# Experts: inner rows weighed and their peaks taken tile by tile without the root, next rows rounded ahead of the results

## The reference, cut to what matters

```python
def rmsnorm(x, w, eps):
    return x * jax.lax.rsqrt(jnp.mean(jnp.square(x), axis=-1, keepdims=True) + eps) * w

def act_quant(x):
    scale = 127.0 / jnp.maximum(jnp.max(jnp.abs(x), axis=-1, keepdims=True), 1e-05)
    return jnp.clip(jnp.round(x * scale), -128, 127) / scale

def bitlinear(x, norm_w, w):
    xn = rmsnorm(x, norm_w, BIT_EPS)          # BIT_EPS = 1e-08
    xq = xn + jax.lax.stop_gradient(act_quant(xn) - xn)
    wq = w + jax.lax.stop_gradient(weight_quant(w) - w)
    return xq @ wq.T

def one_expert(w_col, gpn, gpw, dpn, dpw):
    ...
    h = bitlinear(xin, gpn, gpw)              # 512 rows x 256 -> 512 rows x 1024
    g, y = jnp.split(h, 2, axis=-1)
    out = bitlinear(jax.nn.silu(g) * y, dpn, dpw)   # 512 rows x 512 -> 512 rows x 256
    ...
```

## Time and profile before

| | us |
|---|---|
| median of 3 runs | 2300.96 (2299.19 to 2306.49) |
| the profiled execution | 2308.77 |
| its span | 2307.0 |
| the experts' second block in it, from the first DVE instruction on rows to the next stage | 1573.8 to 1780.2 |
| one expert in its loop, from DVE's L2449 to the next L2449 | 22.55 to 23.04 |
| VectorE busy over the span | 1558.2 (68%) |
| TensorE busy over the span | 1705.8 (74%) |

### The profile page before, as it was taken

One profiled execution on the slowest core, in us unless ns is written; L12 is line 12 of the kernel. 1 busy time (PEld: TensorE's weight loads), 2 busy tenths in 40 slices (PEclk: granted clock), 3 DMA queues, 4 the chain that ended last, 5 costly groups with the idle time before them and its releaser, 6 DMA issues. The chain is left out here.

```text
span 2307.0 us, 43352 instructions
## 1 busy us (share of the span) xinstructions
PE 1705.8 (74%) x13321; PEld 1076.1 (47%) x13338; DVE 1558.2 (68%) x3345; ACT 1437.8 (62%) x2287; POOL 756.4 (33%) x732
## 2 busy tenths in 40 slices
PE   3889898998989998997588882222443687877577
PEld 1456555555555555555376661121222355555323
DVE  6877777777777777774536666644774666766775
ACT  3888889798988888895155566443553332333745
POOL 0434545454554545454000000580000445453000
PEclk9999999999999999998689785555666788989699
DMA  6222222222222222220322110722101301121001
GB/s 185 52 63 54 63 57 58 61 54 63 65 52 63 52 64 59 57 63 17 104 74 74 38 37 21 253 92 91 55 27 58 90 27 31 23 35 19 1 10 65
DMA packets 173814, 139.91 MB, mean 61 GB/s; under 512 B 83794, under 2 KB 155399, under 8 KB 173366
## 3 DMA queue, kind: packets, MB, share of 16 engines
q1 hardware_dynamic: 166710, 122.78, 19.9%
q0 software_dynamic: 6912, 14.71, 2.8%
HBM read 61.92 MB, written 20.97 MB: 36 GB/s over the span
## 5 line engine op out<-in xcount | busy, mean ns | idle before, releaser
L577 ACT ACTIVATE a_p_hi<-ps,a_probs_up,a_s_scale 128x512 f16<-128x512 f32 x512 | 398.0, 777 | 56.0 <-ACTq L575 55.2
L689 DVE TENSOR_REDUCE a_top<-ps 128x2 f32<-128x1024 f32 x256 | 313.2, 1223 | 133.7 <-DVEq L688 133.7
L578 ACT ACTIVATE a_probs<-ps,a_probs_up,a_s_scale 128x512 f32<-128x512 f32 x512 | 398.8, 779 | 0.0
L917 POOL TENSOR_TENSOR a_p_lo<-a_probs,a_p_hi 128x1024 f16<-128x1024 f32 x128 | 276.9, 2163 | 211.8 <-POOLq L916 171.7
L905 POOL TENSOR_TENSOR a_ops<-a_ident_down,a_top 64x256 f16<-64x256 f32 x256 | 159.2, 622 | 344.0 <-POOLq L900 335.4
L441 PE MATMUL ps<-a_ops 128*128 128x512 f16 x512 | 197.8, 386 | 17.8 <-PEq L439 17.7
L698 DVE TENSOR_TENSOR a_p_lo<-a_probs,a_p_hi 128x1024 f16<-128x1024 f32 x128 | 182.9, 1429 | 41.3 <-DVEq L697 41.3
L460 PE MATMUL ps<-a_v_hi,a_p_hi 128*128 128x65 f16 x2048 | 206.4, 197 | 2.2 <-PEq L455 2.2
L463 PE MATMUL ps<-a_v_lo,a_p_hi 128*128 128x64 f16 x2048 | 206.3, 195 | 0.0
L464 PE MATMUL ps<-a_v_hi,a_p_lo 128*128 128x65 f16 x2048 | 206.0, 196 | 0.0
L460 PEld LDWEIGHTS ps<-a_v_hi,a_p_hi 128*128 128x128 f16 x2048 | 191.8, 100 | 23.3 <-issue 12.0
(11 more groups left out here) (493 smaller groups left out, 3750.0 us busy)
## 6 DMA issues: line engine op xcount, KB each, us to landing
a_ops<-a_qk SPq DMA_DIRECT2D x384, 128.0 KB, 2.3
f_w<-in_L_ffn_W_dram SPq DMA_DIRECT2D x16, 1024.0 KB, 7.6
a_qd<-a_qk SPq DMA_DIRECT2D x128, 64.0 KB, 2.2
g_stage<-in_L_attn_gp_w_dram SPq DMA_DIRECT2D x8, 1024.0 KB
X<-in_x_dram SPq DMA_DIRECT2D x8, 512.0 KB, 9.8
expert_in<-g_w SPq DMA_DIRECT2D x8, 512.0 KB
g_stage<-in_L_attn_dp_w_dram SPq DMA_DIRECT2D x8, 512.0 KB
e_x_in<-expert_in SPq DMA_DIRECT2D x8, 512.0 KB, 4.4
```

The lines of the kernel that those rows point to most:

```text
L577: nc.scalar.activation(p_hi[:, h % 2, k, :], scores, ACT.Exp, bias=probs_up[:], scale=s_scale[:])
L578: nc.scalar.activation(probs[:, h % 2, k, :], scores, ACT.Exp, bias=probs_up[:], scale=s_scale[:]).then_inc(st_taken, 1)
L689: nc.vector.tensor_reduce(top[:, c % 2, 2 * pair:2 * pair + 2], ps[:, ROW:ROW + 2, :], AX.X, ALU.max).then_inc(row_taken, 1)
L917: nc.gpsimd.tensor_tensor(p_lo[:, h % 2, 2:KT, :], probs[:, h % 2, 2:KT, :], p_hi[:, h % 2, 2:KT, :], ALU.subtract).then_inc(p_made_pool, 1)
```

## The change

The second `bitlinear`'s norm and quantisation are regrouped. As soon as a tile of `h` is there, VectorE multiplies it by the norm's weights into a new buffer `weighed` and takes its peak, without the root (`weigh`): tiles 0 and 1 together after the first pair, tiles 2 and 3 each after its own `hidden`. In `hidden_rows` the root then enters two small vectors only: the peaks are multiplied by it before the lower bound of 1e-5, and the scale of the rounding is 127 over peak times root. `h` has one buffer for an expert and `weighed` two. On ScalarE, `whole` of the next expert's rows stands ahead of `results`; the rest of `rows_out`, now `rows_turned_out`, stays behind them.

```diff
                     def expert(j, last, first=False):
                         if not first:
-                            whole(r2[:], h[:, (j + 1) % 2], h_round, r2_made)
+                            whole(r2[:], weighed[:, (j + 1) % 2], h_round, r2_made)
...
                         act.drain().then_inc(h_squared_all, 1)
+                        if not last:
+                            whole(r[:], a[:], a_round, r_made)
                         if not first:
                             results((j + 1) % 2)
                         if not last:
-                            rows_out()
+                            rows_turned_out()
                             gate((j + 1) % 2, 0)
                             gate((j + 1) % 2, 1)
...
+                    def weigh(e, j, tiles):
+
+                        dve.drain()
+                        for t in tiles:
+                            nc.vector.tensor_tensor(weighed[:, j, t, :], h[:, t, :], down_n[:, e, :], ALU.mult)
+                        dve.drain()
+                        part = slice(tiles[0], tiles[-1] + 1)
+                        nc.vector.tensor_reduce(h_peak[:, part], weighed[:, j, part], AX.X, ALU.max, apply_absolute_value=True)
+
                     def hidden_rows(e, j):
...
                         rsqrt(nc, dve, rstd[:], value[:], half[:], tmp[:])
+                        nc.vector.tensor_tensor(h_peak[:], h_peak[:], rstd[:], ALU.mult)
+                        dve.drain()
+                        nc.vector.tensor_scalar(h_peak[:], h_peak[:], 1e-5, None, ALU.max)
+                        dve.drain()
+                        nc.vector.reciprocal(per_step[:], h_peak[:])
+                        nc.vector.tensor_scalar(h_step[:, j], h_peak[:], 1.0 / 127.0, None, ALU.mult)
+                        dve.drain()
+                        nc.vector.scalar_tensor_tensor(out=per_step[:], in0=per_step[:], scalar=127.0, in1=rstd[:], op0=ALU.mult, op1=ALU.mult)
+                        nc.vector.tensor_scalar(h_step[:, j], h_step[:, j], mean_of(e, 1), None, ALU.mult)
+                        dve.drain()
                         for t in range(RT):
-                            nc.vector.scalar_tensor_tensor(out=h[:, j, t, :], in0=h[:, j, t, :], scalar=rstd[:, t:t + 1],
-                                                           in1=down_n[:, e, :], op0=ALU.mult, op1=ALU.mult)
-                        dve.drain()
-                        quantise_rows(nc, dve, h[:, j], peak[:], h_step[:, j], per_step[:],
-                                      lambda t: (h[:, j, t, :], per_step[:, t:t + 1]))
-                        nc.vector.tensor_scalar(h_step[:, j], h_step[:, j], mean_of(e, 1), None, ALU.mult)
+                            nc.vector.tensor_scalar(weighed[:, j, t, :], weighed[:, j, t, :], per_step[:, t:t + 1], ROUND, ALU.mult, ALU.add)
                         dve.drain().then_inc(h_round, 1)
 
                     def expert(e, j, last):
                         hidden(j, 0)
                         hidden(j, 1)
+                        weigh(e, j, (0, 1))
                         if not last:
                             rows(e + 1, (j + 1) % 2)
                         hidden(j, 2)
+                        weigh(e, j, (2,))
                         hidden(j, 3)
+                        weigh(e, j, (3,))
                         hidden_rows(e, j)
```

More of the change, by code:

```diff
@@ L2219, in experts @@
             value, half, tmp, rstd, peak, per_step = (sb(n, [P, RT]) for n in ("value", "half", "tmp", "rstd", "peak", "per_step"))
+            h_peak = sb("h_peak", [P, RT])
             h_squares, step, h_step = sb("h_squares", [P, RT]), sb("step", [P, 2, RT]), sb("h_step", [P, 2, RT])
@@ L2222, in experts @@
             a, r, rT = sb("a", [P, RT, D]), sb("r", [P, RT, D], BF16), sb("rT", [P, RT, DC, P], BF16)
-            gated, h = sb("gated", [P, 2, I]), sb("h", [P, 2, RT, I])
+            gated, h, weighed = sb("gated", [P, 2, I]), sb("h", [P, RT, I]), sb("weighed", [P, 2, RT, I])
             r2, r2T = sb("r2", [P, RT, I], BF16), sb("r2T", [P, RT, IC, P], BF16)
@@ L2278, in whole, with rows_turned_out @@
                                              bias=minus_round[:]).then_inc(done, 1)
-                    def rows_out():
-                        whole(r[:], a[:], a_round, r_made)
+                    def rows_turned_out():
                         act.wait_ge(r_turned, 1)
@@ L2290, in gate, with square_hidden @@
                                              scale=step[:, j, t:t + 1]).then_inc(gated_made, 1)
-                    def square_hidden(j, t):
+                    def square_hidden(t):
                         act.wait_ge(h_made, 1)
                         act.sem_inc(h_made, -1)
-                        nc.scalar.activation(junk[:, (t % 2) * I:(t % 2 + 1) * I], h[:, j, t, :], ACT.Square,
+                        nc.scalar.activation(junk[:, (t % 2) * I:(t % 2 + 1) * I], h[:, t, :], ACT.Square,
                                              accum_out=h_squares[:, t:t + 1]).then_inc(h_squared, 1)
@@ L2316, in expert @@
                         if not first:
-                            whole(r2[:], h[:, (j + 1) % 2], h_round, r2_made)
-                        square_hidden(j, 0)
-                        square_hidden(j, 1)
+                            whole(r2[:], weighed[:, (j + 1) % 2], h_round, r2_made)
+                        square_hidden(0)
+                        square_hidden(1)
                         if not first:
@@ L2323, in expert @@
                             gate(j, t)
-                            square_hidden(j, t)
+                            square_hidden(t)
                         act.drain().then_inc(h_squared_all, 1)
+                        if not last:
+                            whole(r[:], a[:], a_round, r_made)
                         if not first:
@@ L2345, in _ @@
                     expert(1, last=True)
-                    whole(r2[:], h[:, 1], h_round, r2_made)
+                    whole(r2[:], weighed[:, 1], h_round, r2_made)
                     hidden_out()
@@ L2442, in hidden @@
                         dve.sem_inc(y_full, -1)
-                        nc.vector.scalar_tensor_tensor(out=h[:, j, t, :], in0=ps[:, G + 1 + 2 * (t % 2), :], scalar=step[:, j, t:t + 1],
+                        nc.vector.scalar_tensor_tensor(out=h[:, t, :], in0=ps[:, G + 1 + 2 * (t % 2), :], scalar=step[:, j, t:t + 1],
                                                        in1=gated[:, t % 2, :], op0=ALU.mult, op1=ALU.mult).then_inc(h_made, 1)
+                    def weigh(e, j, tiles):
[5 more added lines that the diff above has]
+                        nc.vector.tensor_reduce(h_peak[:, part], weighed[:, j, part], AX.X, ALU.max, apply_absolute_value=True)
                     def hidden_rows(e, j):
```

## The result

The changed kernel took 2288.14 us (median of 5 runs, 2285.67 to 2291.41); the kernel before, run beside it, 2306.49 (2299.19 to 2310.24). The ratio is 0.9927, 95% interval 0.9905 to 0.9949, so it is faster by about 17 us. The profiled execution took 2288.14 with a span of 2286.4.

A forecast was written before the change was run, and what follows sets the result against it. VectorE's queue was taken to set the period. The terms 7.1 + 0.7 - 3.6 + 3.6 + 5.0 = 12.8 us won, off 2300.96, gave 2288.2 us, range 2284 to 2297.

The forecast's parts named there:

- case A: In the changed block VectorE stays the bound and the pair waits a few tenths; 10 to 15 us won; chance 0.76.
- The end of an expert: On VectorE, root to first pair shrinks from 11.47 to 6.34 us, 5.1 less.
- The gates: With rounding ahead of results, tile 1's gate is ready at R + 7.15; the pair's second half starts at R + 7.35.
- R: The start of the root's first instruction on VectorE, where the prediction cuts each expert's period.
- rival B: The gates are the bound, the pair's second half starting at R + 8.6; 4 us of gain left, 2297; chance 0.17.
- The hole: VectorE's 1.68 us idle between third and fourth tile: tile 2's weighing, 2.28 in all, fits under the 2.43.
- The multiplication: VectorE's 512-wide product of two SBUF tensors in `weigh`: taken as 0.685 us, bounds 0.68 and 0.75.
- rival D: Wide VectorE work slows while ScalarE squares the same tile, about 1.2 us an expert; 2297; chance 0.03.
- rival C: ScalarE and TensorE's way from `h_round` to the third gate becomes the bound, making the kernel slower; chance 0.04.
- The sum: Over the block: six periods 7.1 and loop edges 0.7 won, head 3.6 lost, last period 3.6 and tail 5.0 won.
- the period: One expert's cycle, R to the next R: 8.1 + 2.85 + 5.54 + 2.43 + 2.45 = 21.4 us against 22.55.
- The clock's side term: If TensorE's eight matmuls ahead of the pair ran at 2.4 GHz, 0.35 us more per period, 2.3 in all.

The follow-up runs named there:

- experiment 4: The changed kernel with tile 2 weighed together with tile 3, behind the fourth product; median 2296.49 us, ratio 0.9952, block 196.15 us.
- experiment 1: The changed kernel with ScalarE rounding the next rows behind the results again; median 2294.68 us, ratio 0.9957, block 199.51 us.
- experiment 5: The changed kernel with tile 2's weighing and its peak done twice; one execution of 2295.13 us, block 201.12 us.
- Experiment 6: The changed kernel with 28 unused matmuls on TensorE ahead of the turn of the next rows; median 2286.44 us, ratio 0.9921, block 189.31 us.
- experiment 7: The changed kernel with GpSimd multiplying the next expert's input rows by the norm's weights; median 2285.35 us, ratio 0.9915.
- experiment 8: The changed kernel with GpSimd multiplying the input rows except the first expert's, each later set started in turn with VectorE; median 2279.41 us, ratio 0.9895.

## Why the prediction was right

The forecast was 2288.2 us in 2284 to 2297, from 12.8 us won; measured were 2288.14, and the block won 16.2. That the two times agree to 0.1 us is luck: the kernel before came out 5.5 us higher in these runs (2306.49) than in the ones shown first (2300.96), and the gain between the medians was larger by as much, 18.4 and not 12.8. The mechanism is the forecast one, but the block's 16.2 lies above the 10 to 15 that case A allowed.

- *The end of an expert*: root to first pair forecast 6.34, measured 6.32 (11.47 before). Two small errors cancel here: with 0.35 of idle time ahead of the pair it is 6.22 (experiment 4), and here the idle time is 0.45; what the 0.10 more waits for is not shown, for the first gate had ended by then (1646.59 + 0.69 = 1647.28).
- *The gates*: the pair's second half at R + 7.35, measured 7.38; experiment 1 shows that the moved rounding is what brings it there; without it rival B's mechanism is what happens (R + 8.86, it said 8.6). B expected 4 us of gain to be left; experiment 1's block keeps 7.4.
- *The hole*: third to fourth product 2.43, measured 2.43; experiments 4 and 5 show that it covers one weighing and no more.
- *The multiplication*: 0.685 taken, 690 ns measured, so rival D is out.
- *The way to the third gate* (rival C): the inner rows' `whole` began at R + 7.05 in the last expert (1733.44), forecast 7.15, and the third tile followed 6.05 later, forecast 6.06. In the loop VectorE waited only 0.34 ahead of the third tile, as before.
- *The sum*, forecast and measured: head 3.6 lost, 3.2 measured (26.96 against 23.75); six periods 7.8 won, 10.2 measured (126.4 against 136.6); last period 3.6, 4.0 measured (17.75); tail 5.0, 5.3 measured.

The mis-sized term is the period, 21.4 forecast and 20.9 to 21.1 in the first five measured. Of the 0.4, 0.24 are in "the same 2.28 and about 0.17 for the wait's own instructions make 2.45": it is 2.21, because with the squares long done the root's first instruction starts 0.09 before the reduction ends (1641.27 + 0.69 against 1641.87). I had charged a gap where there is an overlap. Another 0.12 lie ahead of the next rows (R + 10.83 and not 10.95), where the same happens: they start 0.08 before the reduction ends (1651.56 + 1.22 against 1652.70). My price for the first `weigh` was not even one number: 2.95 ahead of the first root and 2.85 in the period; from the end of the pair to the next rows it measured 2.70.

The clock's side term (2.3 us, if all groups ran at the higher clock) stays open. Experiment 6 gave 1.4, all of it in the last two periods. Inside the loop, where the pair waits for its gate, the eight matmuls did not get the higher clock throughout (3.24 and 3.59 us), and at the edge where they got it nothing was to be won.

## What to carry to other kernels

Look for the wide work that stands between a wait and a signal, and ask whether it needs what is waited for: here a per-row factor could be applied to four elements of a partition in place of 4 x 512, and the wide work moved into the time of the wait. Shortening one arm of a ring pays only as far as the other arm allows, so look what comes second before and after: reordering the other arm was worth 0 alone and 8.8 us together. Compare such changes by the length of the block in the trace: it repeated to 0.1 us where whole times scattered by 10.

## What the runs showed of the hardware

While GpSimd multiplied two SBUF tensors, several of VectorE's smallest TENSOR_SCALAR instructions (128x4) took 0.51 to 0.62 us and not 0.14 to 0.17 (experiments 7 and 8), and two multiplications of SBUF tensors (128x512) took up to 2.31 together and not 1.29 (experiment 7). The reductions beside GpSimd kept their 1.21 to 1.22. In experiment 8 a stretched small one, from 1629.52 on for 0.52, ended as GpSimd's four did (1627.22 + 2.79 = 1630.01).

The Trainium skill (SBUF — State Buffer, Who interferes with whom) says that a VectorE instruction in a mode that uses both ports, or with two SBUF inputs, contends with a GpSimd instruction that reads SBUF, and that the one that comes first holds the shared ports for its whole length. By that rule the wait is up to one GpSimd instruction, here 0.72 us, and the trace agrees: the short ones lost 0.36 to 0.46 each, the two wide ones 1.02 together. That the short ones ran in such a mode is not shown here.

What I had not expected is that the shortest instructions pay too. The wide ones lose more in all, but 0.37 on 0.14 us is several times the instruction, so a chain of small steps is no cheap neighbour for GpSimd.
